# Who rounds the rows to the high part: a second pass of ScalarE over PSUM in place of a cast by VectorE

## The reference, cut to what matters

```python
# graph branch: four experts of two layers each, the best two of them kept by a gate
for e in range(4):
    h = xn
    for l in range(2):
        aggr = segment_sum(h[src], dst) * inv_deg
        h = relu(aggr @ Wl[e, l] + bl[e, l] + h @ Wr[e, l])
# mixer branch, two layers
for i in range(2):
    y = layernorm(x, ln1_g[i], ln1_b[i])
    q, k, v = y @ Wq[i] + bq[i], y @ Wk[i] + bk[i], y @ Wv[i] + bv[i]
    x = x + linear_attention(q, k, v, proj[i]) @ Wo[i] + bo[i]
    y = layernorm(x, ln2_g[i], ln2_b[i])
    h = gelu(y @ W1[i] + b1[i])          # 512 -> 2048
    x = x + h @ W2[i] + b2[i]            # 2048 -> 512
```

## Time and profile before

| what | us |
|---|---|
| median of three runs | 2150.23 |
| lowest and highest | 2143.36, 2153.36 |
| the profiled execution | 2148.25 |
| its span | 2146.4 |
| PE busy (x9514) | 1898.1 |
| DVE busy (x1793) | 898.9 |
| ACT busy (x1170) | 635.6 |
| POOL busy (x520) | 603.3 |
| mean granted clock of TensorE, as a share of full speed | 0.953 |

### The profile page before, as it was taken

One profiled execution on the slowest core, in us unless ns is written; L12 is line 12 of the kernel. 1 busy time (PEld: TensorE's weight loads), 2 busy tenths in 40 slices (PEclk: granted clock), 3 DMA queues, 4 the chain that ended last, 5 costly groups with the idle time before them and its releaser, 6 DMA issues. The chain is left out here.

```text
span 2146.4 us, 28790 instructions
## 1 busy us (share of the span) xinstructions
PE 1898.1 (88%) x9514; PEld 1537.4 (72%) x9515; DVE 898.9 (42%) x1793; ACT 635.6 (30%) x1170; POOL 603.3 (28%) x520
## 2 busy tenths in 40 slices
PE   2677989999999998997999989999889898899992
PEld 1343447888888876785779977888667897678881
DVE  8877611111111123646554546322465454562227
ACT  7622111111111120103634642221165265232210
POOL 0000213232323231204622104433364310064432
PEclk9999999999999999998998999999999799999996
DMA  2010402221312365424731100111157011011111
GB/s 57 1 48 24 133 0 89 75 102 73 107 65 76 112 243 146 136 83 120 202 123 35 54 21 1 40 40 40 38 132 218 27 55 54 1 40 40 40 48 48
DMA packets 75590, 160.31 MB, mean 75 GB/s; under 512 B 9867, under 2 KB 24901, under 8 KB 73707
## 3 DMA queue, kind: packets, MB, share of 16 engines
q1 hardware_dynamic: 75472, 158.80, 23.5%
HBM read 103.24 MB, written 55.53 MB: 74 GB/s over the span
## 5 line engine op out<-in xcount | busy, mean ns | idle before, releaser
L578 PE MATMUL ps<-yT,wslot 128*128 128x500 f32 (+1 forms) x576 | 207.8, 361 | 8.6 <-DVE xm L1779 3.6
L828 PE MATMUL ps<-g,adj 125*128 125x512 f32 (+1 forms) x800 | 191.9, 402 | 18.0 <-DVE o_gnn L975 14.5
L579 PE MATMUL ps<-yT,wslot 128*128 128x500 f32 (+1 forms) x576 | 206.2, 358 | 0.0
L580 PE MATMUL ps<-yT,wslot 128*128 128x500 f32 (+1 forms) x576 | 205.8, 357 | 0.0
L828 PEld LDWEIGHTS ps<-g,adj 125*128 125x128 f32 (+1 forms) x800 | 153.0, 192 | 57.0 <-DVE o_gnn L975 16.9
L1811 POOL TENSOR_TENSOR wslot<-mix_landing,wslot 128x512 fp32r<-128x512 f32 x96 | 128.3, 1368 | 212.3 <-ACT wslot L1471 212.3
L1816 POOL TENSOR_TENSOR hidT<-qpT,hidT 128x500 fp32r<-128x500 f32 (+1 forms) x96 | 103.2, 1078 | 189.6 <-DVE hidT L1642 189.6
L362 PE MATMUL ps<-key_hot,row_hot 125*125 125x500 bf16 x430 | 105.5, 384 | 46.5 <-DVE key_hot L333 36.3
L1535 ACT ACTIVATE qpT<-ps,layer_cols 128x500 f32<-128x500 f32 (+1 forms) x96 | 58.3, 610 | 288.6 <-PE ps L580 244.5
L578 PE MATMUL ps<-parts,w 128*128 128x500 f32 (+1 forms) x384 | 136.1, 355 | 6.1 <-DVE bl L947 6.1
L579 PE MATMUL ps<-parts,w 128*128 128x500 f32 (+1 forms) x384 | 136.1, 354 | 0.0
(11 more groups left out here) (274 smaller groups left out, 3719.8 us busy)
## 6 DMA issues: line engine op xcount, KB each, us to landing
mix_landing<-in_L_mix_W SPq DMA_DIRECT2D x16, 1024.0 KB, 5.2
qk_dram<-qk_parts SPq DMA_DIRECT2D x128, 125.0 KB, 2.4
g_dram<-staged SPq DMA_DIRECT2D x40, 256.0 KB, 2.0
u_dram<-staged SPq DMA_DIRECT2D x40, 256.0 KB, 2.0
g_in<-g_dram SPq DMA_DIRECT2D x40, 256.0 KB, 3.4
u_in<-u_dram SPq DMA_DIRECT2D x40, 256.0 KB, 2.7
k_stack<-qk_dram SPq DMA_DIRECT2D x8, 1250.0 KB, 6.5
q_stack<-qk_dram SPq DMA_DIRECT2D x8, 1250.0 KB, 8.4
```

The costliest lines, as they stand in the source:

```text
L578: nc.tensor.matmul(out, lhs_high, rhs_high, start=first, stop=False)
L579: nc.tensor.matmul(out, lhs_high, rhs_low, start=False, stop=False)
L580: return nc.tensor.matmul(out, lhs_low, rhs_high, start=False, stop=last)
L828: last = nc.tensor.matmul(m.ps[0:counts.shape[1], t % 2, :], counts if exact else counts.bitcast(F32), part if exact else part.bitcast(F32 ...
```

## The change

After the pass that writes the exact rows, ScalarE reads the same PSUM bank a second time with the same function, bias and scale, and writes the high part itself. `h_exact` and `exact_ready` are raised by the second pass. The casts of VectorE at L959 and L1642 are gone, with their semaphores `h_high` and `high_ready`; GpSimd waits for `h_exact` and `exact_ready`. The other casts (L1671 for q and k) stay. The additions of the bias rows `b2` (L1788), which stood between the casts, stay on VectorE without them. ScalarE now writes into `yT`, and gets one wait that no engine had at this place: for `gnn_stored`, once, ahead of the loop over the mixer's layers.

```diff
@@ -856,7 +856,8 @@
                         act.wait_ge(h_summed, e * HN + (n + 1))
                         act.wait_ge(h_low, e * HN + (n + 1))
                         act.wait_ge(bl1_ready, 1)
-                        nc.scalar.activation(tmp[:, n % 2, 0:cn], m.ps[:, n % 4, 0:cn], ACT.Relu, bias=bl1[:, bass.ds(e * K + f, 1)])\
+                        nc.scalar.activation(tmp[:, n % 2, 0:cn], m.ps[:, n % 4, 0:cn], ACT.Relu, bias=bl1[:, bass.ds(e * K + f, 1)])
+                        nc.scalar.activation(hT[:, c % 2, 0, f, 0:cn], m.ps[:, n % 4, 0:cn], ACT.Relu, bias=bl1[:, bass.ds(e * K + f, 1)])\
                             .then_inc(h_exact, 1)
 
                 def stage_g(e, c, last):
@@ -918,7 +919,7 @@
                     for c, (c0, cn) in enumerate(CHUNKS):
                         for f in range(K):
                             n = c * K + f
-                            pool.wait_ge(h_high, e * HN + (n + 1))
+                            pool.wait_ge(h_exact, e * HN + (n + 1))
                             pool.tensor_tensor(hT[:, c % 2, 1, f, 0:cn], tmp[:, n % 2, 0:cn], hT[:, c % 2, 0, f, 0:cn].bitcast(F32),
                                                ALU.subtract).then_inc(h_low, 1)
                     if not last:
@@ -951,13 +952,7 @@
                 vec.sem_inc(u_stored[1], 16)
                 with vec.Fori(0, EXPERTS) as e:
                     for layer, c in ORDER:
-                        c0, cn = CHUNKS[c]
-                        if layer == "first":
-                            for f in range(K):
-                                n = c * K + f
-                                vec.wait_ge(h_exact, e * HN + (n + 1))
-                                nc.vector.tensor_copy(hT[:, c % 2, 0, f, 0:cn], tmp[:, n % 2, 0:cn]).then_inc(h_high, 1)
-                        else:
+                        if layer == "second":
                             if c == 0:
                                 vec.wait_ge(bl2_loaded, e * 16 + 16)
                             for t in TILES[c]:
...
@@ -1485,6 +1480,8 @@
                                 act.wait_ge(low_ready, i * SPLITS + (turn_split(half, n) - 1))
                             bank, to = turn_home(half, n, (t1 - t0) * P)
                             nc.scalar.activation(tmp[:, n % 2, 0:(t1 - t0) * P], m.ps[:, bank, to], ACT.Identity,
+                                                 bias=cols[:, 2 * half + 1, k:k + 1], scale=cols[:, 2 * half, k:k + 1])
+                            nc.scalar.activation(yT[:, 0, k, t0 * P:t1 * P], m.ps[:, bank, to], ACT.Identity,
                                                  bias=cols[:, 2 * half + 1, k:k + 1], scale=cols[:, 2 * half, k:k + 1])\
                                 .then_inc(exact_ready, 1)
 
@@ -1501,6 +1498,7 @@
                     scale_and_shift(2)
 
                 act.wait_ge(eps_ready, 1)
+                act.wait_ge(m.gnn_stored, 32)
                 with act.Fori(0, DEPTH) as i:
                     def project(side, c):
 
@@ -1532,7 +1530,8 @@
                             n = b * HQ + c * K + f
                             act.wait_ge(h_summed, i * QUARTERS * HQ + (n + 1))
                             act.wait_ge(low_ready, i * SPLITS + (hidden_split(n) - 1))
-                            nc.scalar.activation(tmp[:, n % 2, 0:cn], m.ps[:, 4 + n % 4, 0:cn], ACT.Gelu, bias=b1[:, b * K + f:b * K + f + 1])\
+                            nc.scalar.activation(tmp[:, n % 2, 0:cn], m.ps[:, 4 + n % 4, 0:cn], ACT.Gelu, bias=b1[:, b * K + f:b * K + f + 1])
+                            nc.scalar.activation(hT[:, 0, f, c0:c0 + cn], m.ps[:, 4 + n % 4, 0:cn], ACT.Gelu, bias=b1[:, b * K + f:b * K + f + 1])\
                                 .then_inc(exact_ready, 1)
 
                     norm_rows(i, 0, lambda: project(0, 0))
@@ -1637,15 +1636,6 @@
                         nc.vector.tensor_scalar(z[:, t, :], xm[:, t, :], mv[:, t, 0:1], rstd[:, t:t + 1],
                                                 ALU.subtract, ALU.mult).then_inc(z_ready, 1)
 
-                def split_high(i, n, dst, width):
-                    vec.wait_ge(exact_ready, i * SPLITS + (n + 1))
-                    nc.vector.tensor_copy(dst, tmp[:, n % 2, 0:width]).then_inc(high_ready, 1)
-
-                def split_group(i, half, g):
-                    t0, t1 = GROUPS3[g]
-                    for k in range(K):
-                        split_high(i, turn_split(half, g * K + k), yT[:, 0, k, t0 * P:t1 * P], (t1 - t0) * P)
-
                 with vec.Fori(0, DEPTH) as i:
                     norm_group(i, 0, 0)
                     norm_group(i, 0, 1)
...
@@ -1772,28 +1759,22 @@
                     vec.wait_ge(bo_added, i * T + T)
                     vec.wait_ge(o_turned, i * G + G)
                     for g, (t0, t1) in enumerate(GROUPS3):
-                        if g == 2:
-                            split_group(i, 1, 0)
                         for t in range(t0, t1):
                             vec.wait_ge(wo_summed, i * T + (t + 1))
                             nc.vector.tensor_tensor(xm[:, t, :], xm[:, t, :], m.ps[0:P, 6 + t % 2, :], ALU.add).then_inc(wo_added, 1)
                         vec.drain()
                         norm_group(i, 1, g)
-                    def hidden_high(b, c):
-                        c0, cn = CHUNKS[c]
+                    def add_b2(b, c):
                         for f in range(K):
                             n = b * HQ + c * K + f
-                            split_high(i, hidden_split(n), hT[:, 0, f, c0:c0 + cn], cn)
                             if n < T:
                                 nc.vector.tensor_tensor(xm[:, n, :], xm[:, n, :], rows[:, 2, :], ALU.add).then_inc(b2_added, 1)
 
-                    split_group(i, 1, 1)
-                    hidden_high(0, 0)
-                    split_group(i, 1, 2)
+                    add_b2(0, 0)
                     for b in range(QUARTERS):
                         for c in range(len(CHUNKS)):
                             if (b, c) != (0, 0):
-                                hidden_high(b, c)
+                                add_b2(b, c)
                         vec.drain()
                         for t in range(T):
                             vec.wait_ge(ff_summed, i * FT_ALL + (b * T + t + 1))
@@ -1812,7 +1793,7 @@
                     last.then_inc(w_split, 1)
 
                 def split_low(i, n, dst, high, width):
-                    pool.wait_ge(high_ready, i * SPLITS + n + 1)
+                    pool.wait_ge(exact_ready, i * SPLITS + n + 1)
                     pool.tensor_tensor(dst, tmp[:, n % 2, 0:width], high.bitcast(F32), ALU.subtract).then_inc(low_ready, 1)
```

More of the change, by code:

```diff
@@ L654, in stage_experts @@
         w_high, w_split = sem("e_high"), sem("e_split")
-        h_summed, h_exact, h_high, h_low = sem("h_summed"), sem("h_exact_ready"), sem("h_high"), sem("h_low")
+        h_summed, h_exact, h_low = sem("h_summed"), sem("h_exact_ready"), sem("h_low")
         g_summed, g_staged, u_summed, u_staged = sem("g_summed"), sem("g_staged"), sem("u_summed"), sem("u_staged")
@@ L1091, in stage_mixer @@
         var_ready, std_made, z_ready, y_turned = sem("var_ready1"), sem("std_made1"), sem("z_ready"), sem("y_turned")
-        exact_ready, high_ready, low_ready = sem("exact_ready"), sem("high_ready"), sem("low_ready")
+        exact_ready, low_ready = sem("exact_ready"), sem("low_ready")
         qk_summed, qk_copied, v_summed, v_ready = sem("qk_summed"), sem("qk_copied"), sem("v_summed"), sem("v_ready")
@@ L1674, in project_high @@
                                                     square_parts[:, n % SQ_RING, 0, 0:cn].bitcast(F32), ALU.subtract).then_inc(square_low, 1)
-                    split_group(i, 0, 0)
                     norm_group(i, 0, 2)
-                    split_group(i, 0, 1)
                     project_high(0, 0)
-                    split_group(i, 0, 2)
                     project_high(0, 1)
```

## The result

| | median us | lowest, highest | runs |
|---|---|---|---|
| before, beside the changed kernel | 2151.26 | 2143.36, 2155.87 | 6 |
| changed | 2162.91 | 2159.37, 2164.76 | 6 |

The ratio of the changed kernel to the one before is 1.0056, with a 95% interval of 1.0035 to 1.0077. It is slower, by 12 us (7.5 to 16.6 us, the interval times 2151.26). The forecast was 2151, with a range of 2142 to 2160: the time lies outside it, on the slow side. The profiled execution took 2160.87 us, against 2148.25 before.

What follows compares the result with a forecast made beforehand. TensorE was taken as busy throughout experts and feed-forward middle, leaving its waits in norms, first quarter and mixer entry. Terms +7.6 - 0.9 - 2.4 - 1.65 - 0.55 - 1.0 = +1.1 us gave 2151 us, range 2142 to 2160.

Steps and rivals of the forecast that it cites:

- wait at the entry: Mixer entry: ScalarE waits for the store ahead of its table load and first root, paid once, +7.6 us (5.9 to 9.1).
- norm at a layer's start, both layers: From first pass to first product, four chunks finish 0.45 us sooner in each of two layers, -0.9 us together.
- norm before the feed-forward, both layers: Additions to xm no longer stand behind four casts, so TensorE starts W1 1.2 us sooner, twice: -2.4 us.
- first quarter of the feed-forward: Feed-forward's first quarter: GELU and W2 waits shrink, -1.65 us in layer 1 and -0.55 us in layer 0.
- clock at the feed-forward starts: Shorter stalls at the feed-forward starts may spare TensorE's clock falls: -1 us, -5 if both falls go.
- longer fall of the clock at the entry: Mixer entry: TensorE idles longer before the first product; one longer clock fall, only as the clock term's upper bound, +3.4 us.
- bound of +1.1 us: Feed-forward's first quarter, worst case: no saving, and the PSUM bank released later by the second pass, twice.
- shorter chain: One split: two ScalarE passes then the subtraction replace exact rows, cast, subtraction; second pass adds 0.66 us in the norm.
- signs of being wrong: Landing before 990 or after 993.3, subtraction above 1.2 us without the cast, later-quarter exact_ready waits, second pass above 0.7 us.
- second rival: Feed-forward starts: shorter stalls make both clock falls go, sum -2.9 us, 2147.3 us; chance 0.13.
- The experts: Experts' stage: casts leave VectorE and passes come to ScalarE under TensorE's matmuls, cost 0.
- third rival: Behind eight weight blocks, PSUM banks come free 0.57 us too late per chunk: 18.2 us, some 2169.5; chance 0.06.

Runs made afterwards that it cites:

- a_spread: Changed kernel with the ten b2 additions placed one by one, each ahead of its tile's first W2 addition, entry wait kept; 2146.59 us, ratio 0.9988 to before.
- a_drained: Changed kernel with a VectorE drain behind each of the ten b2 additions, still in one block; 2142.79 us in a single execution.
- a_stats: `a_spread` with ten bn_stats, results unused, in the additions' old place; 2144.02 us in a single execution.
- b_spread: Kernel before, casts kept on VectorE, with its b2 additions spread as in `a_spread`; 2145.11 us, ratio 0.9978.
- b_wait: Kernel before with one line more, ScalarE's wait for gnn_stored ahead of the loop over the mixer's layers; 2160.13 us, ratio 1.0051.
- experts_only: Kernel before with the change's edits in the experts' stage and none in the mixer; 2150.84 us, ratio 0.9993.
- a_both: Changed kernel with the gnn_stored wait moved to ScalarE's first write into yT and the b2 additions spread; 2140.32 us, ratio 0.9961 to before.
- a_wait_late: Changed kernel with the gnn_stored wait moved behind the second root, ahead of ScalarE's first write into yT; 2150.62 us, ratio 1.0012 to before.

## Why the prediction was wrong

Its steps in their order, in us, beside what the profiled pair of executions shows:

| step | forecast | measured |
|---|---|---|
| wait at the entry | +7.6 (5.9 to 9.1) | +8.8 |
| norm at a layer's start, both layers | -0.9 | -0.6 (7.06 to 6.73, 7.05 to 6.74) |
| norm before the feed-forward, both layers | -2.4 | -2.9 (8.39 to 6.95, 8.41 to 6.96) |
| first quarter of the feed-forward | -2.2 | +6.7 (2.7 to 9.4) |
| clock at the feed-forward starts | -1.0 (to -5) | -3.1 (-4.8, and +1.7 for the new fall) |
| longer fall of the clock at the entry | 0 (in the bound of +3.4) | +1.0 |
| sum | +1.1 | +9.9 |

The clock's -4.8 is worked out from windows of before, 1316 to 1325 at 0.66 and 1878 to 1888 at 0.83 where the changed kernel has 1.00: 9 x 0.34 + 10 x 0.17. That of the entry: from the first product of the mixer the clock stood at the lower level for 3.4 us before (1001.24 until 0.6 us into the window 1004 to 1014, mean 0.97) and for 5.4 us after (until 1.4 us into the window 1017 to 1027, mean 0.93), half of the difference is lost. The +1.7 is the fall from 1919 to 1923. The runs' +12 us (7.5 to 16.6) has the +9.9 in its interval. Of the 12.6 us between the two profiled executions, 3.3 came ahead of the mixer and are no effect of the change; the 9.3 that are left are 0.6 below the sum. The three rows of the feed-forward (norm, first quarter, clock) come to +0.7, and its two stretches grew by 0.9 us. Attention and the products around it differed by 2 us either way between the same two executions, for no reason found.

**The step that failed** is the one on the first quarter of the feed-forward: "VectorE's ten additions L1788, so far spread between casts, now run in one block and collide with subtractions earlier, where TensorE has spare work." It saw the block and the collision and gave the collision no price; the term came out at +6.7 us where -2.2 was forecast. The price is 7.03 us for a subtraction of 1.2 us, and ScalarE's order hands it on: behind the held subtraction stand four passes (1331.90 to 1333.88), the table load and the first GELU. TensorE had 12 us of work ahead (from 1323.92 to 1335.89, which is 1337.27 less the wait of 1.38), and then needed a bank that the late GELU had not yet freed. The second stall lies further down the same chain: GpSimd starts the low part of the W2 block 23.0 us after the first product of W1 (1346.94), where in `a_spread` it is 18.4 us, and the product at 1354.56 waits for a GELU behind it, 3.31 us against 0.29. In layer 1 the clock fell behind that stall as well, 1.7 us more that no term had. The bound of +1.1 us for this step was 5.6 us too low, since it was made from the second pass's length alone. `a_spread` takes the wait from 9.4 to 0.6 us, `a_drained` to 2.3, and `a_stats` shows that a block of another operation does no harm.

The order of before had the same ten additions with little of this effect (its waits for GELU rows, 2.7 us, go in `b_spread`), and the reason can be seen in the order: each cast waited for ScalarE, so the additions came in ones, with gaps, as they do in `a_drained`. Read together with `a_drained`, the waiting casts that the change removes were what let GpSimd in.

The Trainium skill has a rule for it (SBUF — State Buffer, section SBUF: two separate sides): VectorE and GpSimd share one pair of ports as an exclusive lock; between a VectorE operation with two SBUF inputs and a GpSimd operation that reads SBUF, whichever starts first has it for its whole instruction, and the other engine stands still. The trace agrees in which operations hold and which don't (behind the additions, with two inputs, a subtraction took 7.03 us, beside the `bn_stats` block, with one, the pair took 2.40 us). The rule read literally, one instruction at a time, would have GpSimd held for 0.61 us; here it was held for the whole run of ten, and in between two of them only where a drain stood there (`a_drained`).

**The entry wait** was rightly found and bounded, and 1.2 us too low in size: the store landed 11.6 us after its issue, the one of the earlier trace rows after 10.4. `b_wait` shows it alone: 12.9 us to the root, in the kernel before. Its upper bound took two transfers of one queue to land in the order of their issue, which no row shows; 11.6 us for the store and at most 11.9 for `proj` do not speak against it. The cost was forecast as paid in full, and it was. What the forecast did not ask is whether it had to stand there.

**The shorter chain** came as worked out. The second pass follows the first after 0.65 us in the norm and 0.57 in the GELU (1335.97 to 1336.54), as priced; W1 starts 1.44 us sooner in its norm, against 1.2; TensorE then waits for GpSimd, 0.50 us, in place of VectorE, as the forecast said. One of its signs of being wrong did show: with the cast gone one subtraction of a pair still took 1.26 us (the median of the `yT` view above), where 1.07 had been taken, and the norm at a layer's start gained 0.33 us in place of 0.45. **The clock** went the way of the second rival for this part: both falls of before went, worth 4.8 us of the 5 allowed. That rival (2147.3) needed the first quarter to hold as well, and it didn't, and with its stall came the new fall.

**The experts** at 0 were right, by `experts_only`. The third rival, banks released too late by the second pass, is refuted: with the additions out of the way, TensorE's wait for the second passes of GELU is 0.7 us in `a_both`, far from 18, and for those in the turning 8.7 us, as long as for the exact rows before (8.8).

The forecast gave slower than 0.5% a chance of 0.12, and the highest sum of its bounds was +14.6, so the outcome was inside the bounds and outside the range drawn from them. Two terms at their bad ends at once were left out as unlikely: one was nearly there (+8.8 of 9.1), and one was far beyond it.

## What to carry to other kernels

Before taking instructions off an engine, look at what they kept apart: a step that waits between two others is also a gap, and without it what remains may run as one block against the engine that it used to let in, here GpSimd. An addition that reads two tensors in SBUF is best placed one by one, where the engine waits anyway, and not in a row beside GpSimd's part of a critical chain. And a wait that a change needs for one write belongs right ahead of that write: the same wait cost 8.8 us ahead of a table load and nothing a few instructions later.

## What the runs showed of the hardware

- Beside ten VectorE additions of 0.61 us each, back to back, one GpSimd subtraction took 7.03 us, in both layers (8.06 us for the pair, in both layers of two kernels). Four held the pair for 4.45 us. With a drain behind each addition the engines alternated, 1.41 us for an addition and 1.56 for a subtraction.
- Ten `bn_stats` of 0.60 us, back to back, held it not at all (2.40 us for the pair), and four scalings with one SBUF input by 0.3 us (2.69).
- Two stores of 2.5 MB of the same form landed 10.4 us and 11.6 us after their first issue, the second in two kernels with waits on it (11.6 in both).
- ScalarE's second pass over a bank starts 0.65 us after the first with Identity and 0.57 with GELU, and the one that writes `fp32r` is as long as the other.
- TensorE's granted clock fell to 0.50 behind the feed-forward's start with a stall of 1.79 us ahead of it, also with the additions moved (0.67 over 10 us, `b_spread`), and did not fall behind one of 0.50 us (1.00 in the changed kernel and `a_both`). Behind the stall of 3.31 us it fell in layer 1 of the changed kernel (0.57 over 4 us) and in both layers of `a_wait_late`, but not in layer 0 of the changed kernel, so the length of the stall alone does not settle it.
